# A four-layer graph network on one core: features of the head attention made inside the pairwise attention's loop

## Time and profile before

| | us |
|---|---|
| median of three runs | 12860.74 (12858.55 to 12863.38) |
| profiled execution | 12864.82 |
| its span | 12863.0 |

### The profile page before, as it was taken

How to read it: one execution, slowest core, us unless ns; L and a number is a source line. 1 busy time by engine, 2 the same in 40 slices (tenths; PEclk the granted TensorE clock), 3 DMA queues, 4 the chain that set the end, 5 groups by cost and what they waited for, 6 DMA issues and landing times.

```text
span 12863.0 us, 249907 instructions
## 1 busy us (share of the span) xinstructions
PE 12382.4 (96%) x109953; PEld 6073.2 (47%) x109953; DVE 9744.3 (76%) x13670; ACT 9620.1 (75%) x8537; POOL 377.2 (3%) x588
## 2 busy tenths in 40 slices
PE   7999999999999999999999999999999999999999
PEld 3333743338433384333843348433484334833348
DVE  4888748887588875888758887588875888758886
ACT  3888748877488774887748877488764887658876
POOL 1000000000000000000000000000000000000000
PEclk9999999999999999999999999999999999999999
DMA  2000320003200031000310003100031000310003
GB/s 75 21 18 17 104 79 18 18 17 110 74 18 18 21 115 65 18 18 22 123 56 18 19 22 128 50 18 21 23 130 45 18 21 27 134 37 21 18 27 101
DMA packets 205752, 610.37 MB, mean 47 GB/s; under 512 B 45056, under 2 KB 136832, under 8 KB 139136
## 3 DMA queue, kind: packets, MB, share of 16 engines
q1 hardware_dynamic: 183792, 450.72, 10.2%
q0 software_dynamic: 20880, 143.66, 3.0%
HBM read 556.47 MB, written 8.39 MB: 44 GB/s over the span
## 4 chain that ended last, share of the span: by engine, by line
PE 83%; DVE 13%; ACT 3%; issue 1%; DMA 0%; SPq 0%; POOL 0%; DVEq 0%
PE ps L1169 52%; PE ps L1153 10%; DVE T L853 5%; PE ps L1245 4%; PE ps L1182 4%; PE ps L1318 4%; PE ps L1258 2%; PE ps L1105 2%; ACT T L552 2%; PE ps L1304 2%; DVE E L753 1%; DVE E L754 1%; PE ps L1225 1%; DVE PT L860 1%; DVE adj_ring L845 1%
## 5 line engine op out<-in xcount | busy, mean ns | idle before, releaser
L1169 PE MATMUL ps<-E,a_win 128*32 128x512 f32 x65536 | 7126.7, 594 | 48.3 <-DVE E L755 36.9
L1169 PEld LDWEIGHTS ps<-E,a_win 128*32 128x32 f32 x65536 | 2114.1, 110 | 4879.1 <-issue 4739.0
L525 ACT ACTIVATE E<-Q,ka 128x2048 f32<-128x2048 f32 x2048 | 4073.8, 1989 | 0.0
L753 DVE TENSOR_SCALAR E<-Q,kd 128x2048 f32<-128x2048 f32 x2048 | 2630.9, 1285 | 1013.6 <-PE ps L1169 979.0
L524 ACT ACTIVATE E<-Q,ka 128x1280 f32<-128x1280 f32 x2048 | 2787.3, 1361 | 811.4 <-PE ps L1169 786.1
L754 DVE TENSOR_SCALAR E<-Q,kd 128x2048 f32<-128x2048 f32 x2048 | 2628.8, 1284 | 0.0
L755 DVE TENSOR_SCALAR E<-Q,kd 128x768 f32<-128x768 f32 x2048 | 1259.5, 615 | 0.0
L1245 PE MATMUL ps<-ident,T 128*128 128x128 f32 x8192 | 1112.5, 279 | 120.8 <-ACT T L552 105.4
L853 DVE CUSTOM_DVE_ANT_0 T<-ps,adj_ring 128x2048 f32<-128x2048 f32 x512 | 1172.0, 2289 | 71.9 <-PE ps L1225 70.0
L552 ACT ACTIVATE T<-T,nmin 128x2048 f32<-128x2048 f32 x512 | 1028.6, 2009 | 147.4 <-DVE nmin L853 146.5
L447 ACT ACTIVATE PT<-ps 128x512 f32<-128x512 f32 x1792 | 950.7, 596 | 193.2 <-PE ps L1245 175.2
(11 more groups left out here) (125 smaller groups left out, 7625.4 us busy)
## 6 DMA issues: line engine op xcount, KB each, us to landing
adj_ring<-in_adj SPq DMA_DIRECT2D x384, 1024.0 KB, 5.0
adj_res<-in_adj POOLq DMA_DIRECT2D x128, 1024.0 KB, 6.5
qcur<-AGG SPq DMA_DIRECT2D x896, 16.0 KB, 2.6
qcur<-HT SPq DMA_DIRECT2D x896, 16.0 KB, 2.1
HW<-in_x POOLq DMA_DIRECT2D x9, 1024.0 KB, 7.4
X<-in_x SPq DMA_DIRECT2D x128, 64.0 KB, 2.0
out_x<-X SPq DMA_DIRECT2D x8, 1024.0 KB, 16.5
wq_r<-in_L_gnn_Wq SPq DMA_DIRECT2D x4, 64.0 KB, 2.5
```

The source lines that it names most:

```text
L525: nc.scalar.activation(E[:, s + 3, :], Q2[:, :], ACT.Relu, bias=ka[:, u, 48 + m:49 + m]).then_inc(e_act, 1)
L753: nc.vector.tensor_scalar(E[:, s, :], Q2[:, :], kd[:, u, m:m + 1], 0.0, ALU.add, ALU.max)
L1169: last = mm(ps[QROWS * grp:QROWS * (grp + 1), 4 * u + c, :], win, E[:, s + grp, c * CH:(c + 1) * CH], start=(m == 0), stop=(m == QUADS - 1 ...
```

## The change

- The statistics of layer 2's features are taken tile by tile in the loop of layer 1 (`stats2` and `aggr2`, after quads 14 and 15 of the next tile), normalised into `AGG` instead of `H` (`normal2`, quads 4 to 7 of tiles 5, 9 and 13), put through relu by ACT (`relu2`, quad 10), transposed by PE (`features2`, quad 13, bank 1) and evacuated by ACT to `HT` (`evac_ht2`, quad 15). Tiles 12 to 14 and tile 15 are handled behind the loop.
- The fills have a new order (`FILL_ORDER`): heads 0 to 2 with queries and the keys of chunks 0 to 2, then the keys of chunk 3 for these heads, then head 3. Six stand ahead of the last tile's transposes, four behind its output. Steps 0 and 1 stand behind fills 14 and 19.
- The fills and layer 2's rotating banks move from banks 4 to 7 to 0 to 3, the scores to 4 to 7, and layer 3's banks accordingly (`bank3`); layer 0 of the next batch waits for the last sums of layer 3 before its third chunk.
- `probs_t2` of heads 0 to 2 waits for three exponentials, that of head 3 for the fourth.

```diff
+FILL_ORDER = [(kind, h, max(c, 0)) for h in range(HEADS - 1) for kind, c in (("q", -1), ("k", 0), ("k", 1), ("k", 2))]
+FILL_ORDER += [("k", h, 3) for h in range(HEADS - 1)]
+FILL_ORDER += [("q", 3, 0)] + [("k", 3, c) for c in range(NC)]
+FILL_ORDER += [("v", 0, c) for c in range(NC)] + [("n", 0, c) for c in range(NC)]
+def bank3(t, g):
+    return (4 + (4 * t + g) % 6) % 8
...
 # ACT, tile1
+                    if t in (5, 9, 13) and m == 10:
+                        relu2(b, t // 4 - 1)
+                    if t in (5, 9, 13) and m == 15:
+                        evac_ht2(b, t // 4 - 1, 1)
 # ACT, behind the loop
+                high(b, 0)
+                high(b, 1)
                 exp1(b * NT + NT - 1, 1)
+                high(b, 2)
                 evac1(b * NT + NT - 1, 1)
-                h_section(b, 1, LAYERS, Hf, heads_first)
-                for i in range(5, 10):
+                relu2(b, 3)
+                for i in range(3, 8):
                     high(b, i)
-                for i in range(10, 15):
+                relu2(b, 4)
+                high(b, 8)
+                evac_ht2(b, 3, 5)
+                for i in range(9, 15):
                     high(b, i)
                 step2(b, 1)
                 for i in range(15, 20):
                     high(b, i)
                 step2(b, 2)
 # DVE, tile1
+                    if t in (5, 9, 13) and 4 <= m < 8:
+                        normal2(b, t // 4 - 1, (t - 9 + m,))
+                    if tail and m == 14:
+                        stats2(b, t - 1)
+                    if tail and m == 15:
+                        aggr2(b, t - 1)
+            def stats2(b, t):
+                dve.wait_ge(x2_rdy, b * NT + t + 1)
+                nc.vector.bn_stats(stats[:, t, :], X[:, t, :]).then_inc(ln2_bn, 1)
+            def aggr2(b, t):
+                dve.wait_ge(ln2_bn, b * NT + t + 1)
+                ins = nc.vector.bn_aggr(mv[:, t, :], stats[:, t, :])
+                if any(t == over[-1] for over in G3):
+                    ins.then_inc(ln_stats, 1)
+            def normal2(b, g, over):
+                dve.wait_ge(ln_rstd, b * LN_COUNT + LN_EARLY + g + 1)
+                for t in over:
+                    ins = nc.vector.tensor_scalar(AGG[:, t * D:(t + 1) * D], X[:, t, :], mv[:, t, 0:1],
+                                                  rstd[:, t:t + 1], ALU.subtract, ALU.mult)
+                if over[-1] == G3[g][-1]:
+                    ins.then_inc(z2_rdy, 1)
 # DVE, behind the loop
                 min1(T, 1)
+                normal2(b, 3, G3[3])
+                low(b, 0)
+                low(b, 1)
                 evac1(T, 1)
+                mask2(b, 0)
+                for i in range(2, 6):
+                    low(b, i)
                 finish1(NT - 1, T, 1)
-                dve.wait_ge(x2_rdy, T + 1)
-                for half in range(2):
-                    norm_stats(b, half_of(half), X)
-                for half in range(2):
-                    normalise(b, LN_2, half_of(half), X, H, zn_rdy)
-                mask2(b, 0)
-                for i in range(10):
+                stats2(b, NT - 1)
+                aggr2(b, NT - 1)
+                low(b, 6)
+                low(b, 7)
+                normal2(b, 4, G3[4])
+                for i in range(8, 15):
                     low(b, i)
                 step2(b, 0)
-                for i in range(10, 15):
+                for i in range(15, 20):
                     low(b, i)
                 step2(b, 1)
-                for i in range(15, 20):
-                    low(b, i)
                 step2(b, 2)
 # PE
+                if l == 0 and half == 0 and c == 2:
+                    pe.wait_ge(o3_rdy, b * NT + NT + 3)
+                if m == 0 and T % NT in (6, 10, 14):
+                    pe.wait_ge(ht_sb, (T // NT) * (HTS * NC) + NC + T % NT // 4)
+                    if t in (5, 9, 13) and m == 13:
+                        features2(b, t // 4 - 1, 1, ((t // 4 - 1, chunk_of(t // 4 - 1)),))
+            def features2(b, c, bank, groups):
+                for g, over in groups:
+                    pe.wait_ge(h2_rdy, b * len(G3) + g + 1)
+                    for t in over:
+                        last = nc.tensor.transpose(ps[:, bank, (t % TPC) * P:(t % TPC + 1) * P],
+                                                   AGG[:, t * D:(t + 1) * D], ident[:, :])
+                last.then_inc(ht_ps, 1)
-                if g == 0 and h == 0:
-                    pe.wait_ge(p2_rdy, b * STEPS + (t + 1) * HEADS)
+                if g == 0 and h in (0, HEADS - 1):
+                    pe.wait_ge(p2_rdy, b * STEPS + (t + 1) * HEADS - (h == 0))
 # PE, behind the loop
+                pe.wait_ge(x2_rdy, b * NT + NT - 1)
+                for i in range(6):
+                    fill(b, i)
                 probs_t1(b * NT + NT - 1, 1)
                 out1(b * NT + NT - 1, 1)
-                h_section(b, 1, LAYERS, heads_first)
-                for i in range(5, 10):
+                for i in range(6, 10):
+                    fill(b, i)
+                features2(b, 3, 5, ((3, G3[3]), (4, G3[4])))
+                for i in range(10, 15):
+                    if i == 12:
+                        pe.wait_ge(ht_sb, (b + 1) * (HTS * NC))
                     fill(b, i)
                 step2(b, 0)
-                for i in range(10, 15):
+                for i in range(15, 20):
                     fill(b, i)
                 step2(b, 1)
-                for i in range(15, 20):
-                    fill(b, i)
                 step2(b, 2)
```

More of the change, by code:

```diff
@@ L45 @@
 LN_STEPS += [(i, chunk_of(c)) for c in range(NC) for i in (LAYERS, LN_1)]
-LN_STEPS += [(LN_2, half_of(half)) for half in range(2)]
-LN_STEPS += [(LN_3, over) for over in G3]
+LN_STEPS += [(i, over) for i in (LN_2, LN_3) for over in G3]
 LN_COUNT = len(LN_STEPS)
-LN_EARLY = LN_COUNT - len(G3) - 2
+LN_EARLY = LN_COUNT - 2 * len(G3)
 LN_MID = LN_COUNT - len(G3)
-DVE_STEPS = 59
+DVE_STEPS = 57
 STEPS = NT * HEADS
@@ L501, in high, with relu2, evac_ht2 @@
                 ins.then_inc(f_hi, 1)
+            def relu2(b, g):
+                act.wait_ge(z2_rdy, b * len(G3) + g + 1)
+                cols = AGG[:, G3[g][0] * D:(G3[g][-1] + 1) * D]
+                nc.scalar.activation(cols, cols, ACT.Relu).then_inc(h2_rdy, 1)
+            def evac_ht2(b, c, bank):
+                act.wait_ge(ht_ps, b * (HTS * NC) + NC + c + 1)
+                evac(HT[:, c * CH:(c + 1) * CH], ps[:, bank, :]).then_inc(ht_sb, 1)
             def degrees(b, over):
@@ L625, in _ @@
                 step2(b, 3)
-                for i in range(5 * HEADS + NC, FILLS):
-                    high(b, i)
+                for c in range(NC):
+                    high(b, FILL_INDEX["n", 0, c])
                 for s in range(4, GROUPS + 5):
@@ L831, in low @@
                         bv_b[:, :].rearrange("p (o d) -> p o d", o=1).broadcast_to([P, TPC, D]), ALU.add)
                 else:
-                    c = i - 5 * HEADS - NC
-                    cols = slice(c * CH, (c + 1) * CH)
-                    dve.wait_ge(f_hi, b * (FILLS - NC) + i - NC + 1)
+                    dve.wait_ge(f_hi, b * (FILLS - NC) + high_count(i))
+                if kind == "q":
+                    for rows in (slice(HD, 2 * HD), slice(3 * HD, 4 * HD)):
+                        dst = qcur[rows, 0:2, h, :]
+                        ins = nc.vector.scalar_tensor_tensor(
+                            out=dst, in0=ps[rows, i % 4, 0:2 * P].rearrange("p (u d) -> p u d", u=2),
+                            scalar=bqs_r[rows, h:h + 1], in1=dst.bitcast(F32), op0=ALU.add, op1=ALU.subtract)
@@ L836, in low @@
+                if kind == "k":
+                    dst = kst[2 * HD:P, h, cols]
+                    ins = nc.vector.scalar_tensor_tensor(
+                        out=dst, in0=ps[2 * HD:P, i % 4, :], scalar=bk_r[2 * HD:P, h:h + 1], in1=dst.bitcast(F32),
+                        op0=ALU.add, op1=ALU.subtract)
+                if kind == "n":
                     ins = nc.vector.scalar_tensor_tensor(
@@ L853, in min2 @@
                 nc.vector.tensor_tensor_reduce(
-                    out=T2[:, t % 2, h, :], in0=ps[:, 0:4, :].rearrange("p c n -> p (c n)"), in1=ring[:, t % 2, :],
+                    out=T2[:, t % 2, h, :], in0=ps[:, 4:8, :].rearrange("p c n -> p (c n)"), in1=ring[:, t % 2, :],
                     scale=1.0, scalar=BIG, op0=ALU.add, op1=ALU.min, accum_out=nmin2[:, h:h + 1]
@@ L1224, in scores2 @@
                 for c in range(NC):
-                    last = mm(ps[:, c, :], qcur[:, t % 4, h, :], kst[:, h, c * CH:(c + 1) * CH], start=True, stop=True)
+                    last = mm(ps[:, 4 + c, :], qcur[:, t % 4, h, :], kst[:, h, c * CH:(c + 1) * CH], start=True, stop=True)
                 last.then_inc(s2_ps, 1)
@@ L1303, in transposes3 @@
                         j = g * TPC + k
-                        last = nc.tensor.transpose(ps[:, (4 * t + g) % 6, k * P:(k + 1) * P],
```

(1 more changed line is left out.)

107 lines of the change are left out of this document (44 added, 63 removed).

## The result

The changed kernel takes 12630.1 us, the median of four runs (12628.8 to 12638.6), against 12860.3 for the kernel before in the same job: 230.2 us less, a ratio of 0.982 (95% interval 0.981 to 0.984). The forecast was 12643.

A forecast was written before the change was run, and what follows sets the result against it. PE was taken to bound a batch nearly everywhere. Passage -15.5, exponential's wait -13.0 and loop +1.3 gave -27.2 us a batch, x8 = -218, from 12860.7 to 12643 us; range 12600 to 12725.

The forecast's parts named there:

- Part 1: Pairwise loop: takes over statistics, normalisation, relu and transposes; only PE's added transposes count, 3 x 0.44 = +1.3 us a batch.
- Part 2: Passage between pairwise loop and head attention: new order gains 18.0 us, clock takes back 2.5; -15.5 us a batch.
- its term of +2.5: Passage, late half: PE's idle time brings half clock, costing +2.5 us a batch, bounds 0 and 3.1.
- Part 3: Head attention: PE's wait for the last head's exponential goes in each tile; -13.0 us a batch, bounds -8 and -13.5.
- A: Head attention: DVE becomes the bound, only a quarter of Part 3 is left; 12723 us, chance 0.10.
- B: Passage: gains only half, since ACT and DVE, not PE, carry it; 12703 us, chance 0.12.
- C: Loop: ring runs dry from 1.9 us added lateness, costing up to a quad (3.44 us) a tile; 13048 us, chance 0.04.
- D: Passage stays as long as now and the exponential's wait only moves to head 3; 12850 us, chance 0.03.

The follow-up runs named there:

- experiment 5: Changed kernel with two spare VectorE operations (0.7 us each) added to each tile's statistics in the loop; 12630.7 us.
- experiment 6: Changed kernel with five spare VectorE operations (3.5 us a tile) added to each tile's statistics in the loop; 12796.5 us.
- experiment 10: Changed kernel with the four transposes of H in the loop's tiles 5, 9 and 13 made twice; 12638.0 us.
- experiment 3: Changed kernel with ScalarE's high parts 15 to 19 put ahead of exponential 0 in the passage; 12606.1 us.
- experiment 7: Kernel of experiment 3 with the value fills and their parts moved ahead of step 2; 12599.1 us.
- experiment 4: Changed kernel with fills 0 to 5 and their parts behind the output of tile 15 instead of ahead of its transposes; 12683.3 us.
- experiment 1: Changed kernel with the first chunk's transposes of a tile waiting for all four exponentials again; 12754.7 us.
- experiment 2: Kernel before the change, with only the wait of the exponentials split by head; 12736.0 us.
- experiment 8: Kernel of experiment 7 with VectorE's mask of tile 0 put ahead of an evacuation; 12602.1 us.
- experiment 9: Kernel of experiment 7 with two of the four n fills and their parts moved ahead of step 3; 12591.8 us.

## Why the prediction came out right

**Part 1, the loop: the step was mis-sized, +2.5 instead of +1.3.** The mechanism held: PE's own work alone counts, the ring covers the rest (experiments 5 and 6). The size did not. Twelve quads with the transposes among them take 10.44 + 0.59 + 31.04 = 42.07 us, without them 41.34: 0.73 a place, 2.2 for the three. I had counted only the length of the transposes, 0.44. That part is confirmed by the second four of experiment 10 (0.43). The 0.3 left does not grow with their number nor, by experiment 5, with DVE's work; that it is the price of breaking the stream of 32-column products once is inferred. The last 0.3 us a batch lie in the loop's first 81 us (81.3 on average before, 81.6 after) and are within their scatter; every later tile without these transposes is as long as before (61.47 and 60.87).

**Part 2, the passage: right, -15.4 for -15.5, in part by two errors that cancel.** Minimum 0 starts at T = 23.2 (22.7 was worked out), DVE waits 2.52 us for head 3's queries (2.6), the first transposes of probabilities start 47.4 to 47.6 behind the last product in most batches (48.4). The mean passage is 47.9 where 48.4 was worked out; before, it is 63.25 where the 63.9 of batch 1 was taken for all. The clock falls in all eight batches, but at T = 28 in two only; in the others it stays up through the 3.3 us of idle time there and falls 3 to 7 us later. No run has this passage without a fall, so its term of +2.5 is not confirmed: experiment 3 measured a fall at 2.25 us, less 1.2 at the attention's entry, experiment 7 one at 1.7. Experiment 4 shows that the early fills matter.

**Part 3, the exponential: mis-sized, -16.0 instead of -13.0.** I took the price of the wait from the idle time shown (0.78 in the tile of the earlier trace rows, 13.2 us in the batch). The idle time starts when the last product has ended, but without a wait the next one starts before that end. The wait cost 1.03 us in the tile of experiment 1, and 128 us over the run in both experiments, where 105 were shown in the kernel before and 116 in experiment 1. DVE didn't become the bound. There are two kinds of tile: six in a batch went from 16.90 to 15.81 us (16.03 was worked out), most others from 16.64 to 15.65 (15.86). I had put the first kind down to the statistics of the next batch's features; two of the six have none, and why they are longer stays open. Both kinds are 0.2 shorter than worked out, which is the same error: 1.0 to 1.1 us a tile for the wait, 0.78 to 0.87 shown. A tile of the first kind in batch 1 starts its scores here, and the next one at 2969.99 (experiment 1 has that row):

```profile
2954.18 1.16 PE L1299 MATMUL ps<-kst,qcur 128*128 128x512 f32 x4
```

**Missing terms.** The attention won another 0.9 us a batch, since it starts at full clock (experiments 1 and 2). Layer 3 lost 1.3 a batch. At its entry PE idles 2.3 us in both kernels; in some batches the clock then falls, in others not. Before, batch 1, the first products of layer 3 are slow:

```profile
3170.69 5.33 PE L1318 MATMUL ps<-AGG,H 128*128 128x128 f32 x32 [2.26 <-issue]
```

after, batch 1, they are not:

```profile
3116.78 3.81 PE L1392 MATMUL ps<-AGG,H 128*128 128x128 f32 x32 [2.27 <-issue]
```

That is 1.5 us between batches with the fall and without it, and after the change more batches have it: of the first seven, layer 3 took 86.5 us in five before and in one after, 88 to 89.6 in the others. Three batches after (89.1 to 89.6) have one wait more: PE waits 0.8 to 1.1 us for DVE's operation on `adj_ring`, which has waited over 3 us for the DMA of its row; PE has no such wait before. That the different arrival time decides about the clock is only argued; no experiment took the 2.3 us away.

**The rivals.** A fell by the tiles' 15.81 and 15.65 us; B by the passage; D by both. C fell twice: nothing of PE's time in the loop is a wait beyond those at its start, and its price was wrong, one to one beyond some 2 us and no full quad (experiment 6). With the right price it could have cost 20 us a batch only for 3.5 us of added work.

**The sum.** -218 was predicted. Against the profile's -226: loop +10, exponential -24, clock at the attention's entry -7, layer 3 +10, layer 0 +2, passage +1. That is 8 us net, out of single errors of up to 24 us; that the total came so near is partly luck. The other 5 of the 13 us between forecast and median lie in the profiled execution, the slowest of its four.

The page "TensorE: Matmul & The Clock Gate" of the Trainium skill (Part 4) would have PE's transposes not count as busy for the clock gate. The row of the attention after says otherwise: granted clock 1.00 over 255.7 us in which the transposes of probabilities take about 137 of PE's 252 busy us (1098.6 in eight batches). The measurement decides. The same page (section "Why this matters for your kernels") says that long idle gaps between bursts of products drop the throughput. Experiments 3 and 7 agree for most batches: half clock behind idle times of 3.2 and 3.3 us in five and in seven of eight, at 1.7 to 2.25 us a fall. The same lengths without a fall in the other batches, and the falls behind 1.53 and 2.3 us, show that the length of a gap alone doesn't decide here.

## What to carry to other kernels

The idle time that a profile shows before an instruction understates a wait on PE, because products in a stream overlap: compare the distance of two starts with and without the wait (1.03 against 0.87 here). When independent work fills the gaps of a serial passage, spread it so that no gap is long: moving one wait away made the next one longer, and gave 24 of 44 us, 7 of 27 and nothing (experiments 3, 7, 8), while cutting the last gap in two kept full clock and took 2.0 us off the passage (experiment 9). Then look at what the earlier arrival meets: half of that went into a wait for a DMA. Before extra work is put beside a loop that PE bounds, measure the slack of the ring with a spare operation of known length.

## What the runs showed that was not expected

- An interruption of the 32-column products by four 128-column transposes costs 0.73 us, of which the transposes' own length is 0.44.
- An idle time of 3.17 us in PE was followed by half clock in five batches and not in three (experiment 3), and one of 2.27 at the entry of layer 3 in some batches only. One of 1.53 us at the attention's entry was followed by it in three batches of experiment 3; two of 1.57 and 1.71 us, with products between, in none of eight batches (experiment 9).
- A ring that had been expected to run dry all at once, at 1.9 us of added work, with the loss of a whole quad, took 1.4 us in each tile without a trace in the time and let 1.5 of 3.5 us through.
